# Reopening 14 of 16 stored tile pairs inside the softmax attention instead of in the projection behind it

## The reference

```python
def _L1_attn_ref(x, Wq, bq, Wk, bk, Wv, bv, Wo, bo):   # 16 heads of 16, 4 of keys and values
    scores = jnp.einsum('bghnd,bhsd->bghns', q, k)
    attn = jax.nn.softmax(scores / SCALE, axis=-1)
    out = jnp.einsum('bghns,bhsd->bghnd', attn, v)
    out = out.transpose(0, 3, 1, 2, 4).reshape(B, N, NUM_HEADS * HEAD_DIM)
    return out @ Wo + bo
x = x + _layernorm(_L1_attn_ref(_layernorm(x, axis=-1), ...), axis=-1)
```

## Time and profile before

| | |
|---|---|
| median of 3 runs | 1955.09 us |
| profiled execution: time | 1957.94 us |
| its span, first to last instruction | 1956.2 us |
| mean granted clock of PE | 0.909 |
| busy PE, DVE, ACT | 84%, 74%, 55% of the span |
| softmax attention, exponentials | 904.4 to 1489.8 us |
| projection, first to last instruction | 1494.6 to 1579.4 us |

### The profile page before, as it was taken

The page is one execution under the profiler, slowest core; times in us unless marked ns, Lnnn a source line. Parts: engine busy times, 40 slices in busy tenths (PEclk is TensorE's granted clock), DMA queues, the critical chain, the costliest instruction groups (busy, mean ns, idle before and its releaser), DMA issues. The chain is left out here.

```text
span 1956.2 us, 42086 instructions
## 1 busy us (share of the span) xinstructions
PE 1642.6 (84%) x15122; PEld 943.6 (48%) x15122; DVE 1443.0 (74%) x2806; ACT 1079.1 (55%) x2186; POOL 422.1 (22%) x541
## 2 busy tenths in 40 slices
PE   3987569989999993767999999999997857989950
PEld 2775359966666661221222222222223647977730
DVE  5776877744444446869999999999972987756657
ACT  1444435533333333524999999999995534534422
POOL 3000226611222222220000000000000115834432
PEclk9998669999999996876999999999998958999975
DMA  6700025521111114331121121121003203444445
GB/s 249 281 1 6 1 72 166 171 74 61 58 60 58 61 39 146 117 94 50 36 62 47 36 62 46 37 62 37 18 25 122 85 1 97 140 124 128 128 135 167
DMA packets 113092, 164.47 MB, mean 84 GB/s; under 512 B 20279, under 2 KB 89789, under 8 KB 110589
## 3 DMA queue, kind: packets, MB, share of 16 engines
q1 hardware_dynamic: 97372, 117.85, 20.1%
q0 software_dynamic: 15520, 43.93, 6.0%
HBM read 89.07 MB, written 72.37 MB: 83 GB/s over the span
## 5 line engine op out<-in xcount | busy, mean ns | idle before, releaser
L1511 DVE TENSOR_REDUCE sa_row_max<-psum 128x1 f32<-128x1024 f32 x512 | 582.3, 1212 | 12.0 <-PE psum L1393 11.9
L1494 ACT ACTIVATE sa_probs<-psum 128x512 f32<-128x512 f32 x1024 | 549.6, 597 | 37.7 <-PE psum L1444 28.2
L1393 PE MATMUL psum<-v_k_max,v_q_stack 48*128 48x512 f16 x1024 | 301.4, 398 | 24.1 <-DVE sa_row_max L1511 16.2
L1424 PE MATMUL psum<-sa_probs,sa_v_now 128*32 128x256 f32 (+1 forms) x3840 | 321.0, 406 | 0.1
L1444 PE MATMUL psum<-v_q_stack,sa_k_main 49*128 49x512 f16 x1024 | 309.8, 385 | 1.9 <-ACT sa_probs L1494 1.4
L1988 PE MATMUL psum<-m0w_all,m0fx_xt_high 128*128 x568 | 192.9, 381 | 0.7 <-DVE m0fx_xt_low L1920 0.7
L1444 PEld LDWEIGHTS psum<-v_q_stack,sa_k_main 49*128 49x128 f16 x1024 | 64.6, 94 | 222.1 <-ACT sa_probs L1494 208.7
L1424 PEld LDWEIGHTS psum<-sa_probs,sa_v_now 128*32 128x32 f32 x3840 | 75.7, 108 | 189.9 <-issue 100.1
L1934 DVE TENSOR_TENSOR m0fx_ht_low<-psum,m0fx_ht_high 128x512 f16<-128x512 f32 x71 | 49.1, 692 | 134.4 <-ACT m0fx_ht_high L1902 134.4
L1317 POOL TENSOR_SCALAR sa_max_half<-sa_o_sb 128x128 f16<-128x128 f32 x32 | 9.2, 289 | 553.1 <-ACT sa_o_sb L1485 553.1
L1879 POOL DMA_INDIRECT y_rows<-m0fx_y_sb,m0s_all x71 | 68.1, 959 | 273.2 <-DVE m0fx_y_sb L1941 273.2
(11 more groups left out here) (349 smaller groups left out, 3377.6 us busy)
## 6 DMA issues: line engine op xcount, KB each, us to landing
x_rows<-la_blank SPq DMA_DIRECT2D x18, 1032.0 KB, 8.8
v_q_stack<-q_scratch SPq DMA_DIRECT2D x192, 64.0 KB, 2.4
m0s_all<-x_rows SPq DMA_DIRECT2D x71, 129.0 KB, 2.0
m1fx_x_in<-x_rows SPq DMA_DIRECT2D x71, 129.0 KB, 2.2
m0fs_stage<-in_up SPq DMA_DIRECT2D x16, 512.0 KB, 4.2
m0g_got<-y_rows SPq DMA_DIRECT2D x32, 256.0 KB, 3.9
o_scratch<-sa_o_sb POOLq DMA_DIRECT2D x32, 256.0 KB, 2.5
wo_o_in<-o_scratch SPq DMA_DIRECT2D x32, 256.0 KB, 3.6
```

Source lines behind the costliest of these rows:

```text
L1393: nc.tensor.matmul(mx_ps[m % 2][:, half * 512:(half + 1) * 512], q_stack[h][side:side + ROWS, head, qt * P:(qt + 1) * P], k_max[side:side ...
L1424: last = nc.tensor.matmul(o_ps[32 * g:32 * g + 32, cols], v_now[:, kt, kv, :], probs[(GROUPS * step + g) % 16][:, cols], start=(kt == 0), ...
L1494: nc.scalar.activation(probs[at % 16][:, :], st_ps[bank_of(at)][:, :], ACT.Exp, scale=0.25 / (QK_SCALE * QK_SCALE)).then_inc(s["expd"], 1)
L1511: nc.vector.tensor_reduce(row_max[n % 2][:, at % QT, column:column + 1], mx_ps[m % 2][:, :], AX.X, ALU.max).then_inc(s["maxed"], 1)
```

## The change

Pairs 0 to 13 (units 0 to 6) are opened and normalised in the last two blocks of the attention: their transposes are put behind scores 1 and 2 of steps 242 to 255, four each, into the banks of the maxima. The stored units are loaded into the memory of `q_stack[0]`, which has no more readers by then, two in turn: units 0 and 1 in block 28, the others behind all of SP's other work. DVE normalises them behind its last maximum. The projection starts with turns of pairs that are ready, opens only pairs 14 and 15, with one pair of banks, one reciprocal tile and one loaded unit in place of two, and has 3 banks for turns and for results instead of 2. SP, ACT and DVE begin it in another order.

```diff
+OPENED = 14
 def projected_residual(core, name, wo_dram, bias_row, shared, o_dram=None):
...
-        BANKS = 4 if o_dram is None else 2
+        BANKS = 4 if o_dram is None else 3
...
-            open_ps = [ph.ps(2) for j in range(2)]
-            o_in = [[ph.sb(f"o_in{j}{kv}", [P, 4 * P]) for kv in range(NKV)] for j in range(2)]
-            recip = [ph.sb(f"recip{j}", [P, 2 * HEADS]) for j in range(2)]
-            loaded = [ph.sem(f"loaded{j}") for j in range(2)]
+            open_ps = ph.ps(2)
+            o_in = [ph.sb(f"o_in{kv}", [P, 4 * P]) for kv in range(NKV)]
+            recip = ph.sb("recip", [P, 2 * HEADS])
+            loaded = ph.sem("loaded")
...
             def _(sp):
+                weights.sync_load(sp)
+                bias.sync_load(sp)
                 if o_dram is not None:
-                    for u in range(2 * B):
-                        ge(sp, opened, (u - 1) * 2)
-                        for kv in range(NKV):
-                            sp.dma_start(o_in[u % 2][kv][:, :], o_dram[u, kv, :, :]).then_inc(loaded[u % 2], 16)
-                        if u == 0:
-                            weights.sync_load(sp)
-                            bias.sync_load(sp)
-                else:
-                    weights.sync_load(sp)
-                    bias.sync_load(sp)
+                    for kv in range(NKV):
+                        sp.dma_start(o_in[kv][:, :], o_dram[OPENED // 2, kv, :, :]).then_inc(loaded, 16)
...
                 def open_heads(p):
-                    pe.wait_ge(loaded[p // 2 % 2], (p // 4 + 1) * 16 * NKV)
-                    ge(pe, normalised, p - 1)
+                    pe.wait_ge(loaded, 16 * NKV)
+                    ge(pe, normalised, p - OPENED)
...
                 def turn(p):
-                    if o_dram is not None:
-                        pe.wait_ge(normalised, p + 1)
+                    if o_dram is not None and p >= OPENED:
+                        pe.wait_ge(normalised, p - OPENED + 1)
...
-                if o_dram is not None:
-                    open_heads(0)
-                    open_heads(1)
                 for p in range(LEAD + 1):
                     turn(p)
-                    if o_dram is not None:
-                        open_heads(p + 2)
...
-                    if o_dram is not None and p + LEAD + 3 < PAIRS:
+                    if o_dram is not None and OPENED <= p + LEAD + 3 < PAIRS:
                         open_heads(p + LEAD + 3)
...
             def _(act):
+                raise_high(0)
                 if o_dram is not None:
+                    for p in range(1, LEAD):
+                        raise_high(p)
                     for n in range(shared.PARTS):
                         shared.scalar_high(act, n)
-                raise_high(0)
                 weights.scalar_high(act)
                 bias.scalar_round(act)
...
             def _(dve):
+                lower(0)
                 if o_dram is not None:
+                    for p in range(1, LEAD):
+                        lower(p)
                     for n in range(shared.PARTS):
                         shared.vector_low(dve, n)
-                    for p in range(2):
-                        normalise(p)
-                lower(0)
                 weights.vector_low(dve)
                 bias.vector_rows(dve, core.ident)
-                if o_dram is not None:
-                    normalise(2)
...
                 for step in range(PAIRS + 1):
-                    if o_dram is not None and step + LEAD + 1 < PAIRS:
+                    if o_dram is not None and OPENED <= step + LEAD + 1 < PAIRS:
                         normalise(step + LEAD + 1)
...
 def softmax_attention(core, inputs, v_all, o_dram, coming):
...
+    OPEN_STEP = (BLOCKS - 2) * KT + 2
...
+        stored = q_stack[0][:, :, :].bitcast(F32).rearrange("p (u k h) t -> p u k (h t)", u=2, k=NKV)
+        recip = [ph.sb(f"recip{j}", [P, 2 * HEADS]) for j in range(2)]
...
+        o_again = [ph.sem(f"o_again{j}") for j in range(2)]
...
+                def load_stored(u):
+                    b, h = divmod(u, 2)
+                    ge(sp, s["opened"], (u - 1) * 2)
+                    for j in range(2):
+                        sp.wait_ge(o_out[j], 16 * (u + 1) * NKV // 2)
+                    for kv in range(NKV):
+                        sp.dma_start(stored[:, u % 2, kv, :], o_dram[b, h, kv, :, :]).then_inc(o_again[u % 2], 16)
...
                     if n + 1 < BLOCKS:
                         after_maxima(n + 1)
                         put_maxima(n + 1)
+                    if n == BLOCKS - NKV:
+                        sp.wait_ge(s["scored"], n * BLOCK_EXPS)
+                        for u in range(2):
+                            load_stored(u)
                 coming.sync_load(sp)
+                for u in range(2, OPENED // 2):
+                    load_stored(u)
...
+                def open_heads(p, t):
+                    if t == 0:
+                        pe.wait_ge(o_again[p // 2 % 2], (p // 4 + 1) * 16 * NKV)
+                        ge(pe, s["normalised"], p - 1)
+                    for kv in range(NKV):
+                        at, qt = t * 512 + kv * P, 2 * (p % 2) + t
+                        last = nc.tensor.transpose(mx_ps[p % 2][:, at:at + P],
+                                                   stored[:, p // 2 % 2, kv, qt * P:(qt + 1) * P], core.ident[:, :])
+                    if t == 1:
+                        last.then_inc(s["opened"], 1)
...
                         if g in (1, 2) and halves:
                             maximum(*halves[g + 1])
+                        if g in (1, 2) and 0 <= step - OPEN_STEP < OPENED:
+                            open_heads(step - OPEN_STEP, g - 1)
...
+                for p in range(OPENED):
+                    dve.wait_ge(s["opened"], p + 1)
+                    heads = mx_ps[p % 2][:, :].rearrange("p (h c) -> p h c", c=32)
+                    nc.vector.reciprocal(recip[p % 2][:, :], heads[:, :, DH]).then_inc(s["recip_done"], 1)
+                    dve.wait_ge(s["recip_done"], p + 1)
+                    nc.vector.tensor_tensor(core.y[:, 2 * p:2 * p + 2, :].rearrange("p t (h d) -> p (t h) d", d=DH),
+                                            heads[:, :, 0:DH],
+                                            recip[p % 2][:, :].unsqueeze(2).to_broadcast([P, 2 * HEADS, DH]),
+                                            ALU.mult).then_inc(s["normalised"], 1)
```

More of the change, by code:

```diff
@@ L361, in open_heads @@
                             at, qt = t * 512 + kv * P, 2 * (p % 2) + t
-                            last = nc.tensor.transpose(open_ps[p % 2][:, at:at + P],
-                                                       o_in[p // 2 % 2][kv][:, qt * P:(qt + 1) * P], core.ident[:, :])
+                            last = nc.tensor.transpose(open_ps[:, at:at + P], o_in[kv][:, qt * P:(qt + 1) * P],
+                                                       core.ident[:, :])
                     last.then_inc(opened, 1)
                 def turn(p):
-                    if o_dram is not None:
-                        pe.wait_ge(normalised, p + 1)
+                    if o_dram is not None and p >= OPENED:
+                        pe.wait_ge(normalised, p - OPENED + 1)
                     ge(pe, low, p - BANKS + 1)
@@ L424, in scale @@
                                              bias=shift_y[:, i:i + 1], scale=rstd_y[:, i:i + 1]).then_inc(scaled, 1)
+                raise_high(0)
                 if o_dram is not None:
+                    for p in range(1, LEAD):
+                        raise_high(p)
                     for n in range(shared.PARTS):
                         shared.scalar_high(act, n)
-                raise_high(0)
                 weights.scalar_high(act)
                 bias.scalar_round(act)
-                for p in range(1, LEAD):
-                    raise_high(p)
+                if o_dram is None:
+                    for p in range(1, LEAD):
+                        raise_high(p)
                 for step in range(PAIRS + 1):
@@ L445, in normalise @@
                 def normalise(p):
[L446 to L449, removed]
+                    dve.wait_ge(opened, p - OPENED + 1)
+                    heads = open_ps[:, :].rearrange("p (h c) -> p h c", c=32)
+                    nc.vector.reciprocal(recip[:, :], heads[:, :, DH]).then_inc(recip_done, 1)
+                    dve.wait_ge(recip_done, p - OPENED + 1)
                     nc.vector.tensor_tensor(pair(core.y, p).rearrange("p t (h d) -> p (t h) d", d=DH),
                                             heads[:, :, 0:DH],
-                                            recip[p % 2][:, :].unsqueeze(2).to_broadcast([P, 2 * HEADS, DH]),
+                                            recip[:, :].unsqueeze(2).to_broadcast([P, 2 * HEADS, DH]),
                                             ALU.mult).then_inc(normalised, 1)
@@ L504, in norm_x @@
                     variance(x_halves, core.mean_var[:, :, 0], at, 0.5)
```

(18 more changed lines are left out.)

## The result

The changed kernel takes 1964.69 us (median of 6 runs, 1962.7 to 1965.59) where the kernel before takes 1956.32 (6 runs, 1954.01 to 1959.94): ratio 1.0037, 95% interval [1.0027, 1.0047], so 5 to 9 us slower. The forecast was 1961.6 with a range of 1951 to 1966, and slower with a chance of 0.56.

What follows compares the result with a forecast made beforehand. ACT was taken to set the pace of the last two attention blocks, with PE having only 0.09 us of room per half step. 15.6 - 8.3 - 0.9 - 4.9 + 5.0 = +6.5 us on 1955.09 gave 1961.6, range 1951 to 1966.

Steps and rivals of the forecast that it cites:

- step 1: Last two attention blocks: added transposes lengthen each step from 1.96 to 3.16 us; cost 15.6 us, bounds 6.0 to 18.4.
- 2, head of the projection: Start of the projection: project(0) comes 8.4 us after the stage's start instead of 16.67; gain 8.3 us, bounds 7 to 10.
- Step 3: Projection, project(0) to first addition: pairs without openings save 2.9 us, half clock loses 2.0; gain 0.9, up to 2.9.
- 4, steps 5 to 10: Projection, bound by DVE there: six pairs each lose 0.98 us of reciprocal and product; gain 4.9 us.
- step 5: Projection, pairs 14 and 15 on one pair of banks: PE stands, then works at half clock; cost 5.0 us, bounds 2.7 and 5.5.
- rival (a): Attention: form changes cost nothing or transposes hide better; attention costs 6.0 us, middle of sum -5, 1950; chance 0.25.
- S to T: Last two attention blocks: time from a score matmul's start to the 128x128 fp32 transpose behind it, taken as 0.31 us.
- Rival (b): Projection, head and pair 15: the clock stays up; sum +2.2 us, 1957.3, no measurable change; chance 0.19.
- Rival (c): Attention, PE's queue: waits and loads bite, attention +18.4, one late load +1, sum +10.3, 1965.4; chance 0.10 with another rival.

Runs made afterwards that it cites:

- head_open: The changed kernel with pairs 14 and 15 opened behind the projection's first three turns, into two pairs of banks, and normalised in DVE's step 0; 1.0016 to the kernel before.
- split: The changed kernel with four transposes behind score 0 and four behind score 2, instead of behind scores 1 and 2; ratio 1.0022 to the kernel before.
- one_t: The changed kernel with one transpose in place of four at each place, and without DVE's normalising in the attention; one run, 1975.03 us.

## Why the prediction was right, point by point

| step | predicted | in the trace |
|---|---|---|
| 1, transposes in the attention | +15.6 | +17.5 |
| 2, head of the projection | -8.3 | -8.4 (16.67 to 8.24) |
| 3, to the first addition | -0.9 | -0.3 (16.48 to 16.20) |
| 4, steps 5 to 10 | -4.9 | -5.3 (24.44 to 19.11) |
| 5, pairs 14 and 15 | +5.0 | +5.4 (1.58 to 7.03) |
| behind it, up to the router | 0 | -1.0 |
| sum | +6.5 | +7.9 |

The mechanism came as forecast, step by step, and the sum is 1.4 us too low, since the misses partly cancel: step 1 is 1.9 too low, and the -1.0 behind step 5, which nothing in the prediction foresaw, takes half of it back. (DVE's stands there for ACT, 0.48 and 0.29 us at 1561.55 and 1566.21 in the kernel before, are gone.) Of the 3.1 us between 1961.6 and 1964.69 another 1.2 are in the starting point: 1955.09 was the median of three runs, of six it is 1956.32. The measured time lies near the upper end of the range.

The sign hung on one reading: that PE had 0.09 us of room in a half step beside an ACT that was full. It was right, and rival (a), which needed a step under 2.6 us, fell: the step is 3.28. What was too small in step 1 is the row of four transposes, 0.59 and not 0.54. I took 0.97 for eight less four times 0.11; four of them with the change behind cost 0.15 for the place and not 0.10. That is 13 x 0.1 = 1.3 of the 1.9 us; the stand at pair 4 is 0.3, and the rest the transition S to T, 0.32 for 0.31.

Step 3 assumed that the clock would be at its low level for the first 4 us from project(0) on. It is low for 5.1, up to 1526.4; the first three projects take 8.87 us (1521.28 to 1530.15) and not 8.2. A pair at the full clock is 2.18 (1527.97 to 1530.15) and not 2.07: the 0.97 taken off for eight transposes held a change of form that now stands behind the turn. Windows of the changed kernel:

```profile
1515.00:1516.00 1.00, 0.88 (x5) 0.47 (x3) 0.84 (x2) 0.94 (x2) 0.00 (x0) 0.50 1.00 280
1516.00:1517.00 1.00, 0.00 (x0) 0.00 (x0) 0.96 (x2) 1.00 (x2) 0.00 (x0) 0.91 0.92 274
...
1519.00:1520.00 1.00, 0.00 (x0) 0.00 (x0) 1.00 (x5) 0.25 (x1) 0.00 (x0) 0.80 0.02 8
...
1521.00:1522.00 1.00, 0.72 (x3) 0.25 (x4) 0.63 (x2) 0.00 (x0) 0.00 (x0) 0.50 0.00 0
```

But in between it rose to 1.00 just when PE had nothing to do, and fell again before the projects. Rival (b) was thus nearer than it looked: at the head the clock was at its high level once more, but lost it 1.7 us before project(0). At pair 15 it wasn't; there PE worked at 0.50 after a stand of 7.13 us, as step 5 has it. Step 5's hole is 5.4 us, and head_open, whose stages are 6.9 us shorter without it and the two late normalisings, shows that it could be had back. Rival (c), late loads, is 0.3 us in the changed kernel; it came true in split and one_t, whose steps are shorter, at 2.0 and 2.7 us and more by the clock. I had put unit 2's load out of danger since each unit had over 6 us; it is the weights ahead of the first of them that made it late.

## What to carry to other kernels

Work that is moved beside a stage is free only where its own engine has room. Read that from the starts of its instructions, at a row whose releaser is "issue", and not from busy time or from which engine is full: here two were. Count the changes between tile forms that the new place makes, and don't part instructions that share the array. Eight transposes in one row take 1.02 us and two rows of four 1.18, but the long row won nothing here (a step of 2.99 against 2.96), since a pair of scores behind it took 0.50 us and not 0.31. Best is where the engine stands anyway: here the last store's stand took three pairs for 1.2 us. When an added wait comes earlier by a faster neighbour, its loads must too.

## What the hardware showed that was not expected

- After a stand of 2.7 us PE's granted clock stayed at 0.50 for 45 us of unbroken work (1475.82 to 1521.36) in one_t (one transpose at each place); in split (four) a stand of 2.0 us cost some 7 us at 0.50. Two runs; the cause of the difference is open.
- The clock can rise when the work is over: in the changed kernel it rose to 1.00 at 1516.2, behind 2.8 us of nothing but fp32 transposes (1513.08 to 1515.87) and with PE already idle, fell at 1519.6, and was at 0.50 when work came at 1521.3.
